# Latent attention: exponentials in one fp32 tile of four key tiles, context products on 64-column halves, maxima on 64-row halves

## The reference

```python
q_hk = (hidden_q @ Wq.T).reshape(Bv, Sv, H, K)            # 16 heads
q_big = jnp.einsum('bshk,hkq->bshq', q_hk, w_kc_q)        # 192 wide, then rotary
kv_r = _apply_rope(kv_c, sin_k[None], cos_k[None])
q_r = jnp.einsum('bshq,hqr->bhsr', q_big, W_qr)
k_r = jnp.einsum('bld,hdr->bhlr', kv_r, W_kr)
scores = jnp.einsum('bhsr,bhlr->bhsl', q_r, k_r)
attn = jax.nn.softmax(scores, axis=-1)
ctx_c = jnp.einsum('bhsl,bld->bhsd', attn, kv_r)
ctx_lat = jnp.einsum('bhsd,hkd->bhsk', ctx_c, w_kc_kv)
```

## Time and profile before

| | |
|---|---|
| median of 3 runs | 2302.54 us |
| profiled execution | 2283.25 us, span 2281.4 us |
| weights and layer norm | to about 76 us |
| latent_queries | 76.8 to 303.1 us |
| first batch of latent_attention prepared | to 354.4 us |
| 15 batch periods (transpose to transpose) | 354.4 to 1292.4 us |
| rest of the first attention | to about 1373 us |
| expert blocks and second attention, not changed | from there on |

### The profile page before, as it was taken

The page is one execution under the profiler, slowest core; times in us unless marked ns, Lnnn a source line. Parts: engine busy times, 40 slices in busy tenths (PEclk is TensorE's granted clock), DMA queues, the critical chain, the costliest instruction groups (busy, mean ns, idle before and its releaser), DMA issues. The chain is left out here.

```text
span 2281.4 us, 38538 instructions
## 1 busy us (share of the span) xinstructions
PE 1857.9 (81%) x10550; PEld 1632.6 (72%) x10550; DVE 1492.1 (65%) x2799; ACT 1220.5 (53%) x2996; POOL 1117.1 (49%) x961
## 2 busy tenths in 40 slices
PE   4999958999999999999999973499993689837870
PEld 3677736888888888888888963499993466626870
DVE  4677777777777777767776433377774466656763
ACT  2111115777777767767777851366661266515650
POOL 0455528888788888878888852300004100014005
PEclk9999967999999999999999985699996599958985
DMA  5522251111111111111110002455542100026654
GB/s 159 197 58 57 55 176 55 63 63 63 45 54 63 64 31 63 63 64 63 63 54 11 16 8 78 140 197 196 204 165 58 34 1 0 0 77 196 198 164 113
DMA packets 115748, 195.76 MB, mean 86 GB/s; under 512 B 48213, under 2 KB 94265, under 8 KB 110161
## 3 DMA queue, kind: packets, MB, share of 16 engines
q1 hardware_dynamic: 107409, 180.88, 24.6%
q0 software_dynamic: 8192, 13.15, 2.0%
HBM read 147.01 MB, written 46.63 MB: 85 GB/s over the span
## 5 line engine op out<-in xcount | busy, mean ns | idle before, releaser
L501 POOL TENSOR_TENSOR EL<-E,EH 128x400 fp32r<-128x400 f32 x688 | 833.4, 1239 | 158.5 <-ACT EH L733 154.0
L599 DVE TENSOR_REDUCE PM<-bank 128x1 f32<-128x482 f32 (+1 forms) x624 | 397.2, 650 | 185.9 <-PE bank L578 182.9
L742 ACT ACTIVATE E<-bank 128x400 f32<-128x400 f32 x768 | 386.4, 503 | 212.8 <-PE bank L793 153.2
L733 ACT ACTIVATE EH<-E 128x400 fp32r<-128x400 f32 x768 | 407.0, 532 | 0.0
L175 PE MATMUL bank<-EH,KVH 128*128 128x400 f32 x768 | 283.1, 369 | 19.8 <-POOL EL L501 18.5
L578 PE MATMUL bank<-KH,QS 128*128 128x482 f32 (+1 forms) x624 | 250.9, 414 | 53.9 <-DVE KVL L549 27.6
L1248 POOL DMA_INDIRECT m_back<-rows_out,m_slots x64 | 64.8, 1013 | 450.8 <-DMA rows_out<-m_ys 421.2
L792 PE MATMUL bank<-QS,KH 128*128 128x400 f32 x768 | 272.1, 354 | 14.9 <-issue 9.1
L793 PE MATMUL bank<-QB,KB 66*128 66x400 f32 x768 | 269.1, 350 | 0.0
L175 PE MATMUL bank<-EH,KVL 128*128 128x400 f32 x768 | 265.7, 346 | 0.0
L175 PE MATMUL bank<-EL,KVH 128*128 128x400 f32 x768 | 265.5, 346 | 0.0
(11 more groups left out here) (244 smaller groups left out, 3983.3 us busy)
## 6 DMA issues: line engine op xcount, KB each, us to landing
m_stage_u<-in_m_up SPq DMA_DIRECT2D x20, 1392.0 KB
raw<-in_ctx_T SPq DMA_DIRECT2D x16, 1444.0 KB, 6.1
m_xg<-rows_in SPq DMA_DIRECT2D x55, 256.0 KB, 4.1
rows_out<-m_ys SPq DMA_DIRECT2D x55, 256.0 KB, 3.7
m_stage_d<-in_m_down SPq DMA_DIRECT2D x20, 696.0 KB
queries<-q_out SPq DMA_DIRECT2D x64, 200.0 KB, 2.4
QS<-queries SPq DMA_DIRECT2D x16, 800.0 KB, 6.1
rows_in<-zeros SPq DMA_DIRECT2D x5, 1792.0 KB
```

What stands on the lines that cost most here:

```text
L501: ops.tensor_tensor(EL[:, n % PB, :], E[:, n % EB, :], as_f32(EH[:, n % PB, :]), ALU.subtract).then_inc(sem, 1)
L599: nc.vector.tensor_reduce(PM[:, f:f + 1], psum[F0 + f % f_banks(b)][:, 0:KW[f % KC]], AX.X, ALU.max).then_inc(red_done, 1)
L733: nc.scalar.activation(EH[:, n % PB, :], E[:, n % EB, :], ACT.Copy).then_inc(hi_done, 1)
L742: nc.scalar.activation(E[:, n % EB, :], psum[S0 + n % SB][:, 0:CH], ACT.Exp).then_inc(exp_done, 1)
```

## The change

In words, with the names of the diff:

- The exponentials are kept in fp32 alone, in R. A step now covers 800 columns in two halves (heads of even and of odd number), so a batch has 24 steps (2 groups of 800 columns times 12 key tiles). ScalarE writes R with one instruction of 800 elements from two banks. In R, four key tiles lie side by side for each column, behind a fifth place for a running sum: neighbouring columns of a tile are 5 floats (20 bytes) apart. EH, EL, KVH, KVL and the copies and subtractions that made them are gone.
- The context product is one fp32 product per half with 64 columns of weights (KV), the first half to partitions 0 to 63 and the second to 64 to 127 of one bank.
- The sums no longer come out of that product. VectorE sums the even half over four tiles and the running place (`sum_even`, four instructions of 100 columns per four tiles), GpSimd the odd half one tile at a time (`sum_odd`), and two fp32 products with a matrix of ones per 800 columns add over partitions (`sums`).
- The maximum pieces go in pairs: one on rows 0 to 63 (QS), one on rows 64 to 127 (the high parts, which QB now holds there), in two banks which one VectorE instruction reduces. A pair waits for the reduction of the pair before it.
- TensorE's list is in blocks of two steps: pair, eight score products, pair, four context products of the block before.
- Ten of the key rotation's parts move from VectorE to GpSimd, two stay; the last split of the rows is gone. QB and KB have 128 rows, with zeros and ones set at the start.
- In `latent_queries` M2 is 64 wide, two heads share a bank as two halves, and four DMAs of 64 partitions per pair of heads replace two of 128.

```diff
-                    for half in range(2):
-                        last = nc.tensor.matmul(psum[4 + h % 2][:, 0:CH], M2[:, half, h, :], rot[:, h % TURNS, half, :],
-                                                start=half == 0, stop=half == 1)
+                    for half in range(2):
+                        for o in range(2):
+                            h = 2 * j + o
+                            last = nc.tensor.matmul(psum[4 + j % 2][o * DC:(o + 1) * DC, 0:CH], M2[:, half, h, :],
+                                                    rot[:, h % TURNS, half, :], start=half == 0, stop=half == 1)
...
+        R = fixed(ctx, nc, "R", [P, 2, 2, CH, GT + 1])
+        def tile_of(n, o):
+            return R[:, n // GT % 2, o, :, 1 + n % GT]
...
-            nc.tensor.matmul(psum[F0 + f % banks][:, 0:KW[j]], QS[r][:, t * P:(t + 1) * P],
-                             KH[r][:, sum(KW[:j]):sum(KW[:j + 1])], start=True, stop=True).then_inc(f_ready, 1)
+            if i >= depth:
+                pe.wait_ge(red_done, b_val(b) * NP + (i - depth + 1))
+            for f in pieces(i):
+                t, j = divmod(f, KC)
+                rows = slice((f % 2) * DC, (f % 2 + 1) * DC)
+                high = QB if f % 2 else QS
+                last = nc.tensor.matmul(psum[f_bank(b, i) + f % 2][:, 0:KW], high[r][rows, t * P:(t + 1) * P],
+                                        KH[r][rows, KAT[j]:KAT[j] + KW], start=True, stop=True)
...
+            src = R[:, g % 2, 0, cols, (1 if q == 0 else 0):]
+            nc.vector.tensor_reduce(out, src, AX.X, ALU.add).then_inc(even_sum, 1)
...
+            nc.gpsimd.tensor_tensor(out, first, tile_of(n, 1), ALU.add).then_inc(odd_sum, 1)
...
+            for o in range(2):
+                last = nc.tensor.matmul(psum[MISC][o * DC:(o + 1) * DC, 0:CH], ones[:], ES[:, p, o, :], start=True, stop=True)
...
-                        nc.scalar.activation(E[:, n % EB, :], psum[S0 + n % SB][:, 0:CH], ACT.Exp).then_inc(exp_done, 1)
+                        nc.scalar.activation(tiles_of(n), banks[:, k:k + 2, 0:CH], ACT.Exp).then_inc(exp_done, 1)
...
-                    split_products(nc, psum[A0 + g % 2][:, 0:CH],
-                                   [(KVH[b_mod(b)][:, cols], KVL[b_mod(b)][:, cols], EH[:, n % PB, :], EL[:, n % PB, :])],
-                                   first=t == 0, last=t == KT - 1).then_inc(av_done, 1)
+                    for o in range(2):
+                        last = nc.tensor.matmul(psum[CTX][o * DC:(o + 1) * DC, 0:CH], KV[b_mod(b)][:, t, :], tile_of(n, o),
+                                                start=t == 0, stop=t == KT - 1)
+                    last.then_inc(av_done, 1)
...
+                    v.memset(as_f32(QB[r][DC:, H * S:]), 0.0)
+                    v.memset(as_f32(QB[r][0:DC, :]), 0.0)
...
+                    v.memset(as_f32(KB[r][0:DC, :]), 0.0).then_inc(rows_set, 1)
...
+                    v.memset(as_f32(QB[r][0:1, :]), 1.0)
+                    v.memset(as_f32(KB[r][0:3, :]), 1.0).then_inc(rows_set, 1)
```

More of the change, by code:

```diff
@@ L425, in latent_attention @@
-        KVL = [fixed(ctx, nc, f"KVL{r}", [P, KT * KS + P - KS], F32R) for r in range(BUFS)]
+        KB = [fixed(ctx, nc, f"KB{r}", [P, SKP], F32R) for r in range(BUFS)]
+        KV = [fixed(ctx, nc, f"KV{r}", [P, KT, DC]) for r in range(BUFS)]
         raw = fixed(ctx, nc, "raw", [P, 2, SK])
@@ new lines, in sum_odd @@
+        def sum_odd(pool, b, n):
+            p, t = divmod(n, KT)
+            if t == 0:
+                return
+            pool.wait_ge(exp_done, b_val(b) * NS + (n + 1 + SB))
+            done = b_val(b) * 2 * ADDS + (p * ADDS + t - 1)
+            if t > 1 or p or b is not FIRST:
+                pool.wait_ge(odd_sum, done)
+            if t == KT - 1 and b is not FIRST:
+                pool.wait_ge(sum_done, b_val(b) * 2 + (p - 1))
+            first = tile_of(n - 1, 1) if t == 1 else EA[:]
+            out = ES[:, p, 1, :] if t == KT - 1 else EA[:]
+            nc.gpsimd.tensor_tensor(out, first, tile_of(n, 1), ALU.add).then_inc(odd_sum, 1)
@@ new lines, in sums, with sums_out @@
+        def sums(pe, b, p):
+            pe.wait_ge(even_sum, b_val(b) * NG * PARTS + (2 * PARTS + PARTS * (NG // 2) * (p + 1)))
+            pe.wait_ge(odd_sum, b_val(b) * 2 * ADDS + ADDS * (p + 1))
+            if p == 0 and b is not FIRST:
+                pe.wait_ge(su_done, b_val(b) * 2)
+            for o in range(2):
+                last = nc.tensor.matmul(psum[MISC][o * DC:(o + 1) * DC, 0:CH], ones[:], ES[:, p, o, :], start=True, stop=True)
+            last.then_inc(sum_done, 1)
+        def sums_out(act, b, p):
+            act.wait_ge(sum_done, b_val(b) * 2 + (p + 1))
+            if b is not FIRST:
+                act.wait_ge(sr_in, b_val(b) * 32)
+            nc.scalar.activation(SU[:, p, :], psum[MISC][0:DC + 1, 0:CH], ACT.Copy).then_inc(su_done, 1)
@@ L805, in step @@
-                        if n == TURN_AT and has_next:
+                        if has_next and 2 * m < NP:
+                            max_pair(pe, b + 1, 2 * m)
+                        if m == 0:
+                            if b is not FIRST:
+                                for n in range(NS - 2, NS):
+                                    values(before(b), n)
+                            pe.wait_ge(m_in, b_val(b) * 32 + 32)
+                        for n in (2 * m, 2 * m + 1):
+                            scores(b, n)
@@ L808, in step @@
                             turn_max(pe, b + 1)
-                steps(pe, step)
-                for n in range(NS - BEHIND, NS):
-                    values(Batch(0, B - 1), n)
-                project(pe, Batch(0, B - 1))
+                        for n in (2 * m - 2, 2 * m - 1):
+                            if n >= 0:
+                                values(b, n)
+                        if m == SUM_AT and b is not FIRST:
+                            sums(pe, before(b), 1)
+                        if m == SUM0_AT:
+                            sums(pe, b, 0)
+                        if m == OUT_AT and b is not FIRST:
+                            pe.wait_ge(su_done, b_val(b) * 2 + 1)
+                            project(pe, before(b))
+                steps(pe, step)
+                for n in range(NS - 2, NS):
+                    values(LAST, n)
+                pe.wait_ge(res_done, B - 1)
+                sums(pe, LAST, 1)
+                pe.wait_ge(su_done, 2 * B)
+                project(pe, LAST)
             @block.vector
```

435 lines of the change are left out of this document (221 added, 214 removed).

## The result

The changed kernel takes 2424.05 us (median of 4, 2420.82 to 2427.26) where the kernel before takes 2301.54 (median of 4, 2293.95 to 2312.28): a ratio of 1.0529, 95% interval 1.0484 to 1.0573. The forecast was 2238 us, so its direction was wrong. What happened has the place and nearly the time of rival 3 (2418 us), though not its mechanism, as the experiments show.

A forecast was written before the change was run, and what follows sets the result against it. TensorE was taken to bound the batch, GpSimd close behind. 15 x (59.0 - 62.5) = -52, queries -22, folding -3, start +12, end +1: -64 us, from 2302.5 to 2238 us; own range 2175 to 2290, overall 2160 to 2430.

The forecast's parts named there:

- rival 3: Context: the second half gains nothing because two streams read at 20-byte steps; batch 71.0 us, total 2418; chance 0.17.
- context term: Context products on TensorE: halves overlap, four products in 5 passes of 0.335 us, 20.1 us per batch, before 26.1.
- 56.1 us of TensorE work: TensorE's batch: scores, context, maxima pairs, layout switches, sums by ones, projection and transpose together; before 55.7.
- A1 A2 B1 B2: Assumed order of a context step's passes: A2 beside B1, B2 beside the next A1; 5 passes instead of 8.
- forecast's 59.0: Attention batch in us: TensorE's 56.1 plus 2.9 of waiting, in place of 62.5.
- Pairs and switches: TensorE per batch: 20 maxima pairs at 0.30, 6.0 us, and 44 array layout switches at 0.16, 7.0 us.
- Waiting: TensorE idle per batch: 0.9 us behind VectorE's reductions, 0.5 for rows of maxima, 1.5 for the loop turn.
- Queries -22: latent_queries: a pair of heads takes 5 passes instead of 8, plus two switches; 22 us less.
- folding -3: fold_weights: 64 output columns instead of 128 in 32 products; up to 3 us less.
- The start +12: Before the first batch: VectorE sets more buffer elements, 13 us, one rotation part less gives back 1; 12 us longer.
- Rivals 1, 2 and 4: Overlap without its price, 2170, chance 0.08; GpSimd becomes the bound at `sum_odd`, 2330, 0.09; no halves ever overlap, 2500, 0.13.
- Rival 1: TensorE: half the switches vanish behind loads, pairs cost 0.22; batch 54.5 us, total 2170; chance 0.08.

The follow-up runs named there:

- experiments 1 to 5: Changed kernel with R contiguous, 2142.51 us; one context stream alone, 2408.08; context operand a constant tile stepped by 4, 16, 8 bytes: 2165.51, 2409.24, 2181.35 us.
- contiguous kernel: Changed kernel with R laid out tile by tile, a tile's 400 columns side by side: 2142.51 us, 0.9366 of the kernel before; again 2140.74.
- experiment 2: Changed kernel with only the even half's context product, on 128 weight columns, the odd half's left out: 2408.08 us.
- experiment 9: One chip: contiguous kernel again, 2140.74 us; kernel before with only the changed queries part and folding, 2254.71; three context-copy buffers with division two steps later, 2114.73.
- experiment 6: Contiguous kernel with both context products of a step on all 128 array columns, so no overlap of column halves: 2388.69 us.
- experiment 8: Contiguous kernel with three buffers for the context copy CU: 2175.93 us, 0.9495 of the kernel before.

## Why the prediction was wrong

- **The step that failed is the context term, 20.1 us per batch.** It priced a pass at the 0.335 us of the earlier trace rows, whose operand is contiguous, and let two passes overlap. The overlap came, the price did not hold: couples of 0.72 us at the 20-byte step, 34.6 per batch (experiments 1 to 5). With it, the forecast's own 56.1 us of TensorE work become 70.6, and the measured period is 70.9 with 2.6 of waiting in it, so all else together was over-priced by 2.3. By the distances between starts, pairs and switches took 11.4 us (forecast 13.0), the projection 3.1 (3.5) and the sums by ones 1.5 (2.0).
- **The same step, without the stride, was too dear.** I ordered the passes A1 A2 B1 B2 and got five; they go as A1 B1 A2 B2 and take four, 16.1 us per batch. The contiguous kernel's 55.0 against the forecast's 59.0 looks like exactly this 4.0, but that is partly luck: projection and sums came out 0.9 cheaper there, and the waits 0.8 dearer (3.7 for 2.9).
- **Rival 3** named the 20-byte step, and 71.0 us per batch, 2418. Its mechanism was half wrong: it let the second half gain nothing at 0.335 a pass (32.2 us), while in truth the halves gain fully at 0.72 (34.6). Two errors that nearly cancel; a single stream (experiment 2) tells them apart. I had given it 0.17, because no row showed a stepped operand. The cachelines rule that the prediction quoted beside it (the Trainium skill, "SBUF — State Buffer") was the better witness: it wants two hits per 16-byte line, and 8 bytes cost 0.02 us per pass while 16 bytes doubled it. A change that lays four key tiles side by side for each column should have made that its first question.
- **Pairs and switches** were right in sum for the contiguous kernel. Scores, pairs and switches of a block: 4.05 us from pair to pair in the contiguous kernel, less 1.34 of context and 1.45 of scores, leaves 1.26; the prediction had 2 x 0.30 + 4 x 0.16 = 1.24. Over a batch they are 12.9 against 13.0. Single gaps differ, if a pair is 0.22: 0.1 into a pair from scores, 0.2 on either side of the context, and 0.3 from a pair to scores, of which 0.1 lies behind the first score product.
- **The other engines.** Pair reduction 1.16 us (forecast 1.15; the 1136 ns above are a mean with 16 single pieces in it), `sum_odd` 1.252 (1.26), VectorE 40.6 busy per batch (43; that was called "as before", but the earlier trace rows has 46.8), GpSimd 42.6 (43.6). `sum_even` 0.56 and 0.665 (0.56 and 0.67). The exponential was 1.65 us for 0.88: its write at the 20-byte step doubles it, a second place where I priced the operation by a contiguous row. It was hidden, since ScalarE had only 40.3 us in 71.6.
- **Waiting** was forecast at 2.9 us per batch and is 2.6, but 1.2 of it is one that I did not name, the context behind the copy of the sums.
- **Outside the periods.** Queries -22 and folding -3: together they bring the first transpose forward by 21.3 us (experiment 9), for a forecast of 25. Folding ended 2.2 us sooner, at 66.2 for 68.4, but the first product with M starts at 80.2 where it was 80.0. latent_queries ended 25.7 us earlier on TensorE (four passes per pair, not five). The start +12: with the contiguous kernel's attention behind the same queries the first transpose stands at 345.7, 12.6 later than 333.1; in the changed kernel VectorE's settings take 27.3 us (285.04 to 312.35) where they took 12.5. Together -9 to -10, forecast -13. The sentence that the first pieces should start near 340 us did not follow from these terms, which give 331.2 - 25 + 12 = 318; they start at 322.1:

```profile
322.10 0.74 PE L575 MATMUL banks<-KH,QS 64*128 64x482 f32 x1 [43.85 <-DVE KB L548]
```

- **Rivals 1, 2 and 4.** GpSimd bound nothing: it was busy 42.6 of 71.6 us and sat idle for ScalarE's R (345.6 us in the page's group above). That no halves overlap is refuted by experiment 6. Rival 1 is refuted too: it had pairs and switches at 7.9 us, and even the contiguous kernel has 12.9. (Its own sum is off by 0.6: 51.0 of work and 2.9 of waiting are 53.9, not 54.5.)

## What to carry to other kernels

A layout change can move the time of every engine that touches the tile (here three lost and one gained), and a row from a contiguous operand is no price for a stepped one: if no row has the step, give the worst end real weight, or ask for the layout that keeps TensorE's operand contiguous and lets the one reader that wants the other order take the step. When two cases give nearly the same total, choose an experiment on their mechanism (one stream instead of two), not on the total. And a wait that is taken away moves everything behind it: look at what the engines did in the gap that it made. And judge such a change by its single batches too: the mean period of 56.6 us in experiment 8 hid batches of 53.9 and of 59.

## What the runs showed of the hardware

- fp32 products of 400 columns, operand stepped by 4, 8, 16 and 20 bytes: eight records in two streams in 1.56, 1.63, 3.02 and 3.06 us. One stream stepped by 20 bytes: four records in 3.10.
- Two fp32 products on different 64-column halves interleave their passes and start 6 to 10 ns apart, in latent_queries too, where eight records that stood in 2.85 us now stand in 1.56:

```profile
183.85 1.56 PE L321 MATMUL banks<-rotated,M 96*64 96x400 f32 x8
```

- ScalarE writing 800 elements from PSUM: 0.84 us contiguous, 1.65 at a 20-byte step. GpSimd's sum of 400: 1.04 and 1.25. VectorE's reduction over four or five places: 0.56 and 0.665 us innermost, 0.84 and 1.02 at 1600 bytes.
- VectorE's product of two SBUF operands (800 elements): 0.97 us alone. Beside GpSimd either it waits (4.6 us, behind three GpSimd instructions in a row) or GpSimd's sum does (1.9 us in place of 1.04).
- TensorE after 4.5 us of standing still: granted clock 0.51 over the next 6 us, where the contiguous kernel has 1.00.
